# Four engine queues reordered around the attention add of a convolution-attention block with a quantised FFN, on one Trainium2 core

## The chip, the cores and the metric

One core of a Trainium2 chip runs the kernel. The time is device time in microseconds (us) of one execution, compared as a median over runs. In a profile, PE is TensorE, PEld its weight loads, DVE VectorE, ACT ScalarE, POOL GpSimd and SP the queue that issues the DMAs. Each engine works through its own list of instructions in order; semaphores join the lists.

## The reference

The input x is (16, 512, 24, 8): images, channels, rows, columns. Two blocks follow each other, each with a layer norm and a residual.

```python
def reference(x, fc1_w, fc2_w, sa_w, w1, w2):        # w1, w2: 2048 x 512 and 512 x 2048
    x = x + conv_attention(ln_over_channels(x))      # block 1
    t = tokens(x)                                    # (16, 192, 512)
    t = t + ffn(ln_over_last(t))                     # block 2
    return images(t)

def conv_attention(v):
    ca = sigmoid(mlp(mean_hw(v)) + mlp(max_hw(v)))   # mlp(a) = relu(a @ fc1.T) @ fc2.T
    v = v * ca                                       # gate of each channel
    s = conv7x7(concat(mean_c(v), max_c(v)), sa_w)
    return v * sigmoid(s)                            # gate of each token

def bitlinear(a, w):                                 # ternary weights, activations in 8 bits
    scale = 127 / max(max_abs_last(a), EPS)
    return (clip(round(a * scale)) / scale) @ ternary(w).T

def ffn(a):
    return bitlinear(gelu(bitlinear(a, w1)), w2)
```

## The kernel before

Two images make a pair: 384 tokens, three tiles of 128 tokens. There are eight pairs (NP = 8), and the loop's body c runs four stages of four pairs at once: FFN of `pair` = c (last tile) and of `nxt` = c + 1 (first two tiles), the normalisation of `nxt`, the channel and token gates of `att` = c + 2, and the turn into tokens and first statistics of `fresh` = c + 3. Bodies 0 to 4 have all of it; body 5 has no `fresh`, body 6 no `att` either, body 7 only the FFN of the last pair. A part before the loop prepares the weights and the first pairs.

The order of the work is written out by hand, once for each engine, in a `body` of each engine's block (POOL L513, ACT L695, DVE L1036, PE L1327). Nothing is reordered at run time. In one body the queues hold, in this case's names:

- DVE: `token_gate` and, for each tile of `nxt`, `add_attention` (L851: t = pv * gate + xt at L856, then statistics at L858 and L860) and `centre` (L862: cen = t - mean at L868, its largest magnitude at L869, then three tiny steps that need `rs2`, the reciprocal deviation that POOL makes, and give `q1`). For each tile `hidden_max` reads the Gelu's output twice, in halves (L883), `hidden_scale` makes `q2` (L891, L893), and `add_ffn` (L900) adds the FFN's product to t. For `att`: four `token_max` (L795), `hidden` (L802, L805) between the two small matrix products, `split_gate` (L815 to L818), three `scale_channels` (L824), `split_stats` (L837, L838) and, after the convolution on PE, `sum_conv` (L843). For `fresh`: `channel_stats` (L782) and `aggregate` (L788).
- POOL: `rstd2` (L452, L453) makes rs2; `round_x` (L477, L481) rounds cen once q1 is there; `round_g` (L488, two halves of 1024 columns, and L494) rounds the Gelu's output once q2 is there; `normalise1` (L458 to L466) makes v1 of `fresh` once DVE has aggregated its statistics.
- ACT: Gelu in four blocks of 512 columns, `pack_g` to f16 (two halves; after each SP issues a transposing DMA into hq), `token_mean` (after token_max), `copy_xq`, the two tanh gates, `sum_channels` (needed by split_stats) and copies out of PSUM. All its work is in the profile at L550.
- PE: `ffn_in` (L1190, four blocks of four 512-column matmuls), `ffn_out` (L1201, four quarters of four), the transposes `turn_x` (L1110), `turn_v1` (L1120), `turn_xq` (L1175, needs cen rounded) and `turn_res` (L1210), the small products `fc1` (L1130, needs all token_max and token_mean), `fc2` (L1136, needs `hidden`), `turn_ca` (L1143), `spread_ca` (L1152), and `conv` (L1166, 42 matmuls of 3 columns, needs split_stats).

In DVE's code a `link` issues an instruction and then waits for its end, a `chain.mark` only counts it, and `chain.wait()` waits for all counted ones:

```python
link(dve.scalar_tensor_tensor(t_tile, pv[par][:, s, :], sg[par][:, s:s + 1],   # L856
                              xt[par][:, s, :], ALU.mult, ALU.add))
link(dve.bn_stats(st2[:, :], t_tile))                                          # L858
wait(dve, rs2_ready, tile.at(1, -1))
dve.bn_aggr(mv2[tile.par][:, :], st2[:, :]).then_inc(stats2_ready, 1)          # L860
```

Of the kernel before, what the change touches and what calls it, by code (L numbers as in the profile page):

```python
# [5 lines left out]
def metaformer_kernel(nc, x, fc1_w, fc2_w, sa_w, w1, w2, out):  # L6
# [38 lines left out]
    with ctx:  # L45
# [340 lines left out]
        def _(pool):  # L386
# [126 lines left out]
            def body(pair, attend, normalise, turn, split):  # L513
# [6 lines left out]
                if normalise:  # L520
                    round_x(Tile(nxt, 0))
                round_g(Tile(pair, 2))
                if normalise:
                    rstd2(Tile(nxt, 1))
                    round_x(Tile(nxt, 1))
                    round_g(Tile(nxt, 0))
                    rstd2(Tile(nxt, 2))
                    round_x(Tile(nxt, 2))
# [12 lines left out]
        def _(act):  # L541
# [153 lines left out]
            def body(pair, attend, normalise, turn):  # L695
# [31 lines left out]
                if normalise:  # L727
                    gelu(Tile(nxt, 1), blocks=(0, 1))
                if attend:
                    copy_caT(att)  # L730
                if normalise:
                    gelu(Tile(nxt, 1), blocks=(2, 3))
# [5 lines left out]
                copy_out(Tile(pair, 1), OUT_BANK[2])  # L738
                if attend:
                    sum_channels(Tile(att, 2))  # L740
                if turn:
# [11 lines left out]
        def _(dve):  # L753
# [95 lines left out]
            def add_attention(tile):  # L849
# [6 lines left out]
                link(dve.scalar_tensor_tensor(t_tile, pv[par][:, s, :], sg[par][:, s:s + 1],  # L856
                                              xt[par][:, s, :], ALU.mult, ALU.add))
                link(dve.bn_stats(st2[:, :], t_tile))  # L858
# [141 lines left out]
            add_attention(Tile(pair0, 0))  # L1000
            centre(Tile(pair0, 0))
# [8 lines left out]
            add_attention(Tile(pair0, 1))  # L1010
            dve.wait_ge(w_turned, 8)
# [14 lines left out]
            add_attention(Tile(pair0, 2))  # L1026
            centre(Tile(pair0, 2))
# [8 lines left out]
            def body(pair, attend, normalise, turn):  # L1036
                nxt, att, fresh = pair.plus(1), pair.plus(2), pair.plus(3)

                if pair.c > 0:
                    add_ffn(Tile(pair.plus(-1), 2))  # L1040
                if normalise:
                    token_gate(nxt)
                    add_attention(Tile(nxt, 0))
                    centre(Tile(nxt, 0))
# [6 lines left out]
                hidden_scale(Tile(pair, 2))  # L1051
                if attend:
                    token_max(att, 2, V1_BANK[2])

                add_ffn(Tile(pair, 0))
                if normalise:
                    add_attention(Tile(nxt, 1))
# [3 lines left out]
                if normalise:  # L1061
                    hidden_max(Tile(nxt, 0), 0)
                    hidden_max(Tile(nxt, 0), 1)
                if attend:
                    hidden(att)
# [4 lines left out]
                if normalise:  # L1070
                    add_attention(Tile(nxt, 2))
                if attend:
                    split_gate(att)
                if normalise:
                    centre(Tile(nxt, 2))
                    hidden_max(Tile(nxt, 1), 0)
# [3 lines left out]
                if turn:  # L1080
                    channel_stats(fresh, 0, 1)
# [336 lines left out]
```

## Time and profile before

| | us |
|---|---|
| median of 3 runs (lowest, highest) | 311.19 (310.03, 312.21) |
| the profiled execution's own time | 311.29 |
| its span, first to last instruction | 309.3 |
| busy in the span: PE, DVE, ACT, POOL | 265.9, 249.7, 217.1, 165.6 |

The 2.0 us between the span and the execution's time lie outside the instructions. Rows of the trace are told in us from the span's start. A timeline row gives start, length, engine, line, operation, output and input, how many instructions it merges, and in brackets how long the engine had idled and who released it. An instruction's length on DVE or POOL contains any time in which it has begun and can't go on.

### The profile page before, as it was taken

The numbers are of one execution on the slowest core, as the hardware profiler recorded it, in microseconds if no ns is written. First come the engines' busy times: TensorE is split into PE (matmuls) and PEld (weight loads), VectorE is DVE, ScalarE is ACT, GpSimd is POOL, SyncE is SP. The second block draws the span as 40 slices with busy tenths as digits, with TensorE's granted clock in tenths as the row PEclk, the third lists the DMA queues.
The fourth block names the chain that finished last, engine by engine and source line by source line (L and its number), as shares of the span: only waits on it lengthen the run. The fifth ranks groups of instructions, "written<-read, shape, count | busy, mean of one in ns | idle before, by whom it ended". The sixth has DMA issues, their size and how long they took to land.

```text
span 309.3 us, 5830 instructions
## 1 busy us (share of the span) xinstructions
PE 265.9 (86%) x1826; PEld 153.4 (50%) x1834; DVE 249.7 (81%) x556; ACT 217.1 (70%) x442; POOL 165.6 (54%) x267
## 2 busy tenths in 40 slices
PE   2457659696699999999999999999999987999974
PEld 2345634564356465645565555555555544444431
DVE  0673889989699989998998999899989997788410
ACT  1863687579476978687778876787678846676831
POOL 9506655416855385648555765566656563346410
PEclk9999965969999999999999999999999999899998
DMA  7999100002253129412931393439223713073693
GB/s 202 389 392 401 45 1 0 2 2 57 42 141 70 24 46 246 96 34 54 252 72 35 69 237 70 37 69 256 53 50 72 151 39 68 17 174 72 74 209 102
DMA packets 71077, 34.19 MB, mean 111 GB/s; under 512 B 52040, under 2 KB 68424, under 8 KB 70536
## 3 DMA queue, kind: packets, MB, share of 16 engines
q1 hardware_dynamic: 69300, 32.78, 43.1%
q10 hardware_dynamic: 1748, 1.05, 1.2%
q8 instruction: 15, 0.25, 0.3%
q14 instruction: 14, 0.11, 0.1%
HBM read 14.94 MB, written 6.29 MB: 69 GB/s over the span
## 4 chain that ended last, share of the span: by engine, by line
DVE 40%; PE 36%; issue 10%; ACT 4%; POOL 4%; ACTq 2%; DMA 1%; another core or an unknown queue 1%; SPq 1%; DVEq 0%; POOLq 0%
PE ps_o L1201 12%; DVE amax L883 8%; PE ps_h L1190 6%; PE ps_t L1190 6%; DVE t L856 6%; PE front L1120 3%; DVE st L858 3%; DVE amax L869 3%; DVE pv L824 3%; PE small L1166 2%; DVE cen L868 2%; DVE junk_v L909 2%; DVE st L782 2%; PE front L1210 2%; DVE res L900 2%
## 5 line engine op out<-in xcount | busy, mean ns | idle before, releaser
L1201 PE MATMUL ps_o<-w2T,hq 128*128 128x512 f16 x384 | 92.7, 379 | 1.1 <-DMA hq<-w_raw 1.1
L488 POOL TENSOR_SCALAR w_room<-w_room,q 128x1024 f32<-128x1024 f32 x48 | 57.1, 1201 | 51.4 <-DVE q L893 50.9
L883 DVE TENSOR_REDUCE amax<-w_room 128x1 f32<-128x1024 f32 (+1 forms) x48 | 57.2, 1208 | 2.3 <-ACT w_room L550 2.2
L1190 PE MATMUL ps_h<-w1T,xq 128*128 128x512 f16 x208 | 54.0, 403 | 1.1 <-ACT xq L550 0.7
L1201 PEld LDWEIGHTS ps_o<-w2T,hq 128*128 128x128 f16 x384 | 36.3, 98 | 36.0 <-DMA hq<-w_raw 2.1
L550 ACT ACTIVATE w_raw<-w_room 128x1024 f16<-128x1024 f16 x48 | 50.4, 1052 | 0.6 <-POOL w_room L488 0.6
L550 ACT ACTIVATE w_room<-ps_h,s 128x512 f32<-128x512 f32 x52 | 35.0, 688 | 13.1 <-PE ps_h L1190 12.0
L1190 PE MATMUL ps_t<-w1T,xq 128*128 128x512 f16 x176 | 42.0, 382 | 0.0
L550 ACT ACTIVATE w_room<-ps_t,s 128x512 f32<-128x512 f32 x44 | 30.2, 687 | 8.0 <-PE ps_t L1190 5.6
L1190 PEld LDWEIGHTS ps_h<-w1T,xq 128*128 128x128 f16 x208 | 20.1, 103 | 23.9 <-issue 3.9
L550 ACT ACTIVATE junk_m<-front 128x192 bf16<-128x192 f32 x64 | 20.6, 332 | 14.7 <-DVE pooled L795 14.7
L900 DVE SCALAR_TENSOR_TENSOR res<-ps_o,s,t 128x512 f32<-128x512 f32 x24 | 18.0, 749 | 13.4 <-PE ps_o L1201 13.4
L477 POOL TENSOR_SCALAR cen<-cen,q 128x512 f32<-128x512 f32 x24 | 16.6, 692 | 20.4 <-DVE q L875 20.4
L1190 PEld LDWEIGHTS ps_t<-w1T,xq 128*128 128x128 f16 x176 | 17.1, 99 | 20.0 <-issue 1.1
L856 DVE SCALAR_TENSOR_TENSOR t<-pv,sg,xt 128x512 f32<-128x512 f32 x24 | 26.3, 1094 | 0.3
L1110 PE MATMUL front<-id,x_in 128*128 128x128 f32 x96 | 17.0, 314 | 7.7 <-DMA x_in<-in_x 5.8
L1120 PE MATMUL front<-id,v 128*128 128x128 f32 x96 | 18.2, 312 | 5.9 <-POOL v L465 3.8
L782 DVE BATCH_NORM_STATS2 st<-xt 128x6 f32<-128x512 f32 x24 | 15.5, 681 | 8.3 <-ACT xt L550 8.3
L550 ACT ACTIVATE w_room<-front 128x512 f32<-128x512 f32 x24 | 14.0, 585 | 8.8 <-PE front L1210 8.8
L795 DVE TENSOR_REDUCE pooled<-front 128x2 f32<-128x384 f32 x32 | 17.7, 552 | 2.5 <-PE front L1120 1.6
L465 POOL TENSOR_SCALAR v<-xt,minus_mean,rs 128x512 f32<-128x512 f32 x24 | 18.9, 788 | 1.4
L550 ACT ACTIVATE junk_p<-pv 128x512 bf16<-128x512 f32 x24 | 15.0, 626 | 6.0 <-DVE ch_stat L824 5.2
(125 smaller groups left out, 450.5 us busy)
## 6 DMA issues: line engine op xcount, KB each, us to landing
out<-w_room SPq DMA_DIRECT2D x16, 384.0 KB, 3.0
x_in<-in_x SPq DMA_DIRECT2D x14, 384.0 KB, 5.1
w_room<-in_L_ffn_w SPq DMA_DIRECT2D x4, 1024.0 KB, 8.8
w_raw<-in_L_ffn_w SPq DMA_DIRECT2D x4, 1024.0 KB, 12.0
x_in<-in_x ACTq DMA_DIRECT2D x2, 384.0 KB, 3.8
hq<-w_raw SPq DMA_TRANSPOSE x48, 3.1
fc_raw<-in_L_conv_fc_w ACTq DMA_DIRECT2D x2, 128.0 KB, 4.2
taps_rev<-in_L_conv_sa_w SPq DMA_DIRECT2D x1, 0.2 KB
```

What stands on the lines that cost most here:

```text
L465: pool.tensor_scalar(v1[:, s, :], xt[pair.par][:, s, :], minus_mean[:, s:s + 1], rs1[:, s:s + 1], ALU.add, ALU.mult).then_inc(normed, 1)
L488: pool.tensor_scalar(part, part, q2[tile.par][:, 0:1], MAGIC, ALU.mult, ALU.add).then_inc(g_rounded, 1)
L550: act.activation(out_ap, in_ap, func, **more).then_inc(signal, 1)
L782: chain.mark(dve.bn_stats(st1[:, s, :], xt[pair.par][:, s, :]))
L795: dve.tensor_reduce(pooled[:, k, 0:2], front[bank][:, 0:TOK].rearrange("p (i t) -> p i t", i=2), AX.X, ALU.max).then_inc(max_ready, 1)
L856: link(dve.scalar_tensor_tensor(t_tile, pv[par][:, s, :], sg[par][:, s:s + 1], xt[par][:, s, :], ALU.mult, ALU.add))
L883: chain.mark(dve.tensor_reduce(amax2[:, i:i + 1], w1_room[:, first + i * F // 2:first + (i + 1) * F // 2 + i], AX.X, ALU.max, apply_absolu ...
L900: dve.scalar_tensor_tensor(res[tile.par][:, :], ps_o[:, :], s2[tile.third][:, 0:1], t[tile.pair.par][:, tile.s, :], ALU.mult, ALU.add).the ...
L1110: last = pe.transpose(front[bank][:, tile_cols(k)], x_in[tile.pair.par][:, k, tile_cols(tile.s)], id32[:, :])
L1120: last = pe.transpose(front[bank][:, tile_cols(s)], v1[:, s, tile_cols(k)], id32[:, :])
L1190: last = pe.matmul(banks[b], xq[tile.pair.par][:, tile.s, k, :], w1T[:, k, b * 512:(b + 1) * 512], start=(k == 0), stop=(k == NC - 1))
L1201: last = pe.matmul(ps_o[:, :], hq[tile.par][:, k, :], w2T[:, k, :], start=(k == 0), stop=(k == NF - 1))
```

## The change

No instruction is added or taken away; their places in the four lists change, and DVE's attention add is split in two.

- `add_attention` only issues the add, counted and not waited for; its statistics become a step of their own, `row_stats`.
- DVE: the add of nxt's tile 1 goes from behind `hidden_scale(pair, 2)` and `add_ffn(pair, 0)` to ahead of both, with token_max 2 between it and its statistics; the add of tile 2 goes from behind `hidden_scale(nxt, 0)` to behind token_max 3, ahead of `hidden`, its statistics behind `hidden`, ahead of the second hidden_max of (nxt, 0). Of that tile's two hidden_max the first now goes ahead of `centre(nxt, 1)`. `split_gate` goes ahead of `hidden_scale(nxt, 0)`; scale_channels 0 and 1 go ahead of hidden_max(nxt, 1, 0), scale 2 ahead of channel_stats; `split_stats` goes ahead of hidden_max(nxt, 1, 1) and its scale; `add_ffn(pair, 2)` goes from the head of the next body to this body's end, ahead of aggregate(fresh, 2).
- POOL: rstd2 of tiles 1 and 2 go ahead of the round_g that stood before them.
- ACT and PE: two small steps trade places with a Gelu block, a copy, a block of ffn_in or a quarter of ffn_out. `turn_xq(nxt, 2)` on PE now stands behind the last quarter of ffn_out(pair, 2).

The diff, with some lines of context left out:

```diff
 # POOL, body
                     round_x(Tile(nxt, 0))
+                    rstd2(Tile(nxt, 1))
                 round_g(Tile(pair, 2))
                 if normalise:
-                    rstd2(Tile(nxt, 1))
                     round_x(Tile(nxt, 1))
+                    rstd2(Tile(nxt, 2))
                     round_g(Tile(nxt, 0))
-                    rstd2(Tile(nxt, 2))
                     round_x(Tile(nxt, 2))
 # ACT, body
-                    gelu(Tile(nxt, 1), blocks=(0, 1))
+                    gelu(Tile(nxt, 1), blocks=(0,))
                     copy_caT(att)
-                    gelu(Tile(nxt, 1), blocks=(2, 3))
+                    gelu(Tile(nxt, 1), blocks=(1, 2, 3))
                     sum_channels(Tile(att, 0))
                     sum_channels(Tile(att, 1))
                     pack_g(Tile(nxt, 0), 0)
+                    sum_channels(Tile(att, 2))
                 copy_out(Tile(pair, 1), OUT_BANK[2])
-                    sum_channels(Tile(att, 2))
 # DVE, add_attention
-                link(dve.scalar_tensor_tensor(t_tile, pv[par][:, s, :], sg[par][:, s:s + 1],
-                                              xt[par][:, s, :], ALU.mult, ALU.add))
-                link(dve.bn_stats(st2[:, :], t_tile))
+                chain.mark(dve.scalar_tensor_tensor(t_tile, pv[par][:, s, :], sg[par][:, s:s + 1],
+                                                    xt[par][:, s, :], ALU.mult, ALU.add))
+
+            def row_stats(tile):
+
+                chain.wait()
+                link(dve.bn_stats(st2[:, :], t[tile.pair.par][:, tile.s, :]))
                 wait(dve, rs2_ready, tile.at(1, -1))
                 dve.bn_aggr(mv2[tile.par][:, :], st2[:, :]).then_inc(stats2_ready, 1)
 # DVE, body
-                if pair.c > 0:
-                    add_ffn(Tile(pair.plus(-1), 2))
                     token_gate(nxt)
                     add_attention(Tile(nxt, 0))
+                    row_stats(Tile(nxt, 0))
                     centre(Tile(nxt, 0))
 ...
                 hidden_max(Tile(pair, 2), 1)
+                    add_attention(Tile(nxt, 1))
+                    token_max(att, 2, V1_BANK[2])
+                    row_stats(Tile(nxt, 1))
                 hidden_scale(Tile(pair, 2))
-                    token_max(att, 2, V1_BANK[2])
 
                 add_ffn(Tile(pair, 0))
-                    add_attention(Tile(nxt, 1))
+                    hidden_max(Tile(nxt, 0), 0)
                     centre(Tile(nxt, 1))
                     token_max(att, 3, V1_BANK[3])
-                    hidden_max(Tile(nxt, 0), 0)
+                    add_attention(Tile(nxt, 2))
+                    hidden(att)
+                    row_stats(Tile(nxt, 2))
                     hidden_max(Tile(nxt, 0), 1)
-                    hidden(att)
+                    split_gate(att)
                     hidden_scale(Tile(nxt, 0))
 
                 add_ffn(Tile(pair, 1))
-                    add_attention(Tile(nxt, 2))
-                    split_gate(att)
                     centre(Tile(nxt, 2))
-                    hidden_max(Tile(nxt, 1), 0)
                     scale_channels(Tile(att, 0), CA_BANK[0])
                     scale_channels(Tile(att, 1), CA_BANK[1])
+                    hidden_max(Tile(nxt, 1), 0)
+                    scale_channels(Tile(att, 2), CA_BANK[2])
                     channel_stats(fresh, 0, 1)
-                    scale_channels(Tile(att, 2), CA_BANK[2])
                     aggregate(fresh, 0, 1)
+                    split_stats(att)
                     hidden_max(Tile(nxt, 1), 1)
                     hidden_scale(Tile(nxt, 1))
-                    split_stats(att)
                     channel_stats(fresh, 2)
                     sum_conv(att)
+                add_ffn(Tile(pair, 2))
                     aggregate(fresh, 2)
 # PE, body
-                    ffn_in(Tile(nxt, 1), blocks=(0, 1))
+                    ffn_in(Tile(nxt, 1), blocks=(0,))
                     turn_ca(att)
-                    ffn_in(Tile(nxt, 1), blocks=(2, 3))
+                    ffn_in(Tile(nxt, 1), blocks=(1, 2))
                     a = spread_ca(Tile(att, 0), CA_BANK[0], a)
                     b = spread_ca(Tile(att, 1), CA_BANK[1], b)
+                    ffn_in(Tile(nxt, 1), blocks=(3,))
                 ffn_out(Tile(pair, 2), (0,))
 ...
                     b = turn_x(Tile(fresh, 2), X_BANK[2], b)
+                ffn_out(Tile(pair, 2), (3,))
                     a = turn_xq(Tile(nxt, 2), XQ_BANK[2], a)
-                ffn_out(Tile(pair, 2), (3,))
                     conv(att)
```

## Rows read from the trace of the kernel before

**Rows 1.** The page: busy time of the engines, and the chain that ended last

```profile
PE 265.9 (86%) x1826; PEld 153.4 (50%) x1834; DVE 249.7 (81%) x556; ACT 217.1 (70%) x442; POOL 165.6 (54%) x267
...
DVE 40%; PE 36%; issue 10%; ACT 4%; POOL 4%; ACTq 2%; DMA 1%; another core or an unknown queue 1%; SPq 1%; DVEq 0%; POOLq 0%
```

**Rows 2.** Stretches of bodies 1 to 5; busy us by engine, then granted clock

```profile
109.58:139.86 30.28, 29.44 (x210) 16.75 (x209) 28.34 (x64) 23.73 (x52) 18.21 (x31) 1.00 0.47 105
...
230.70:262.02 31.32, 28.48 (x198) 15.33 (x197) 28.00 (x59) 22.41 (x49) 17.50 (x28) 1.00 0.41 81
```

**Rows 3.** Timeline of VectorE, body 3

```profile
170.17 0.17 DVE L843 TENSOR_REDUCE conv_sum<-small 128x3 f32<-128x9 f32 x1 [0.72 <-PE small L1166]
...
172.95 0.52 DVE L868 TENSOR_SCALAR cen<-t,mv 128x512 f32<-128x512 f32 x1
...
174.80 0.55 DVE L795 TENSOR_REDUCE pooled<-front 128x2 f32<-128x384 f32 x1
...
179.22 0.74 DVE L900 SCALAR_TENSOR_TENSOR res<-ps_o,s,t 128x512 f32<-128x512 f32 x1
179.88 1.56 DVE L856 SCALAR_TENSOR_TENSOR t<-pv,sg,xt 128x512 f32<-128x512 f32 x1
...
184.28 0.55 DVE L795 TENSOR_REDUCE pooled<-front 128x2 f32<-128x384 f32 x1
...
188.25 1.17 DVE L856 SCALAR_TENSOR_TENSOR t<-pv,sg,xt 128x512 f32<-128x512 f32 x1
...
196.73 0.24 DVE L788 BATCH_NORM_AGGREGATE mv<-st 128x2 f32<-128x6 f32 x2
...
198.67 0.46 DVE L838 TENSOR_TENSOR ch_stat<-ch_stat 128x6 f32<-128x6 f32 x1
```

**Rows 4.** Timeline of GpSimd, body 3

```profile
170.77 0.19 POOL L458 TENSOR_SCALAR ve<-mv 128x1 f32<-128x1 f32 x1
...
173.27 0.59 POOL L453 TENSOR_TENSOR rs<-ve,half_pow 128x1 f32<-128x1 f32 x1
...
178.69 2.21 POOL L488 TENSOR_SCALAR w_room<-w_room,q 128x1024 f32<-128x1024 f32 x2 [2.46 <-DVE q L893]
...
187.76 2.64 POOL L488 TENSOR_SCALAR w_room<-w_room,q 128x1024 f32<-128x1024 f32 x2 [2.37 <-DVE q L893]
...
199.86 1.11 POOL L488 TENSOR_SCALAR w_room<-w_room,q 128x1024 f32<-128x1024 f32 x1
```

**Rows 5.** Timeline of VectorE, before the loop

```profile
40.33 0.70 DVE L868 TENSOR_SCALAR cen<-t,mv 128x512 f32<-128x512 f32 x1
```

**Rows 6.** Timeline of TensorE, body 3

```profile
185.69 0.61 PE L1130 MATMUL small<-pooled,fc1T 128*64 128x4 f32 x8
...
199.19 0.61 PE L1166 MATMUL small<-ch_stat,band 128*128 128x3 bf16 x18 [0.37 <-DVE ch_stat L838]
```

**Rows 7.** Timeline of VectorE, end of body 5

```profile
258.64 1.01 DVE L837 TENSOR_TENSOR ch_stat<-ch_stat 128x6 f32<-128x6 f32 x1 [0.22 <-ACT junk_p L550]
259.68 1.06 DVE L838 TENSOR_TENSOR ch_stat<-ch_stat 128x6 f32<-128x6 f32 x1
```

**Rows 8.** Timeline of GpSimd, end of body 5

```profile
258.51 2.21 POOL L488 TENSOR_SCALAR w_room<-w_room,q 128x1024 f32<-128x1024 f32 x2 [4.23 <-DVE q L893]
```

**Rows 9.** Timeline of TensorE, bodies 5 to 7

```profile
260.80 0.61 PE L1166 MATMUL small<-ch_stat,band 128*128 128x3 bf16 x18 [1.41 <-DVE ch_stat L838]
...
261.88 3.22 PE L1190 MATMUL ps_h<-w1T,xq 128*128 128x512 f16 x8
264.90 2.29 PE L1190 MATMUL ps_t<-w1T,xq 128*128 128x512 f16 x8
...
285.18 0.39 PE L1175 MATMUL front<-id,cen 128*128 128x128 f16 x4
...
286.27 1.89 PE L1190 MATMUL ps_h<-w1T,xq 128*128 128x512 f16 x8
```

**Rows 10.** A stretch of 1 us in body 6, columns as in rows 2

```profile
263.00:264.00 1.00, 1.00 (x3) 0.30 (x2) 0.96 (x2) 0.56 (x1) 0.00 (x0) 0.50 0.06 16
```

More of the change, by code:

```diff
@@ L737, in body @@
                     pack_g(Tile(nxt, 0), 0)
-                copy_out(Tile(pair, 1), OUT_BANK[2])
                 if attend:
                     sum_channels(Tile(att, 2))
+                copy_out(Tile(pair, 1), OUT_BANK[2])
                 if turn:
@@ L1000, in _ @@
             add_attention(Tile(pair0, 0))
+            row_stats(Tile(pair0, 0))
             centre(Tile(pair0, 0))
@@ L1010, in _ @@
             add_attention(Tile(pair0, 1))
+            row_stats(Tile(pair0, 1))
             dve.wait_ge(w_turned, 8)
@@ L1026, in _ @@
             add_attention(Tile(pair0, 2))
+            row_stats(Tile(pair0, 2))
             centre(Tile(pair0, 2))
@@ L1050, in body @@
                 hidden_max(Tile(pair, 2), 1)
-                hidden_scale(Tile(pair, 2))
+                if normalise:
+                    add_attention(Tile(nxt, 1))
                 if attend:
                     token_max(att, 2, V1_BANK[2])
+                if normalise:
+                    row_stats(Tile(nxt, 1))
+                hidden_scale(Tile(pair, 2))
                 add_ffn(Tile(pair, 0))
                 if normalise:
-                    add_attention(Tile(nxt, 1))
+                    hidden_max(Tile(nxt, 0), 0)
                     centre(Tile(nxt, 1))
@@ L1061, in body @@
                 if normalise:
-                    hidden_max(Tile(nxt, 0), 0)
+                    add_attention(Tile(nxt, 2))
+                if attend:
+                    hidden(att)
+                if normalise:
+                    row_stats(Tile(nxt, 2))
                     hidden_max(Tile(nxt, 0), 1)
                 if attend:
-                    hidden(att)
+                    split_gate(att)
                 if normalise:
@@ L1070, in body @@
                 if normalise:
-                    add_attention(Tile(nxt, 2))
-                if attend:
-                    split_gate(att)
-                if normalise:
                     centre(Tile(nxt, 2))
-                    hidden_max(Tile(nxt, 1), 0)
                 if attend:
@@ L1079, in body @@
                     scale_channels(Tile(att, 1), CA_BANK[1])
-                if turn:
-                    channel_stats(fresh, 0, 1)
+                if normalise:
+                    hidden_max(Tile(nxt, 1), 0)
                 if attend:
@@ L1084, in body @@
                 if turn:
+                    channel_stats(fresh, 0, 1)
                     aggregate(fresh, 0, 1)
+                if attend:
+                    split_stats(att)
                 if normalise:
@@ L1088, in body @@
                     hidden_scale(Tile(nxt, 1))
-                if attend:
-                    split_stats(att)
                 if turn:
@@ L1099, in _ @@
                 body(Pair(c), c < NP - 2, c < NP - 1, c < NP - 3)
-            add_ffn(Tile(Pair(NP - 1), 2))
         @block.tensor
@@ L1379, in body @@
                     b = spread_ca(Tile(att, 1), CA_BANK[1], b)
+                if normalise:
+                    ffn_in(Tile(nxt, 1), blocks=(3,))
                 ffn_out(Tile(pair, 2), (0,))
```

## The prediction

> **What bounds the kernel now.** I began with the page's chain of work that ended last: DVE has 40% of it and PE 36% [rows 1], so no single engine sets the time. The stretches by body say why. A full body takes 30.28 us, with DVE busy 28.34 and PE 29.44 in it; bodies 1 to 4 are alike within 0.02, so the loop is steady, and only body 5 is longer, 31.32 [rows 2]. PE's busy time covers waits between pipelined matmuls, so I read the timelines next, of body 3, and looked for lengths that the work doesn't explain. The reader should see three things there. DVE's only marked idle time is 0.72 before sum_conv, where it waits for the convolution, whose own start waited 0.37 for DVE's split_stats [rows 3, 6]. The add of attention takes 1.56 for tile 1 and 1.17 for tile 2, though add_ffn, as many elements with one operand in PSUM, takes 0.74 [rows 3]. Both lie beside a round_g of GpSimd (178.69 to 180.90, 187.76 to 190.40), and the second add stretches that round_g from 2.21 to 2.64 in return [rows 4]. So the add and a GpSimd instruction over SBUF exclude each other: the later one waits for the other's end. The add's 1.56 ends 0.54 behind round_g's end, so 0.54 is what it needs once let in.
>
> **What one full body saves.** The add of tile 1 moves ahead of hidden_scale(pair, 2), which releases the first round_g: 1.56 - 0.74 = 0.82. That of tile 2 moves ahead of hidden_scale(nxt, 0): 1.17 - 0.74 = 0.43. split_stats moves ahead of a hidden_max, so the POOL work that stretched L838 to 0.46 [rows 3] comes later; a tiny step such as sum_conv takes 0.17: 0.29. The wait before sum_conv, 0.72, goes, since hidden_max, hidden_scale and channel_stats now stand between split_stats and it. In four places the queue no longer waits for its last instruction to end (two adds, the hidden_max ahead of the first of them, statistics of tile 1). Unlinked, add_ffn lets its successor start 0.66 behind its own start, 0.08 before it ends [rows 3]; with the restart I take 0.11 each, 0.45. Sum: 2.71.
>
> **What the same body pays.** Five new waits, in the order of DVE's queue.
>
> First, centre of nxt's tile 0 needs rs2. GpSimd works from the statistics of fresh's first tiles (196.73 + 0.24 [rows 3]) to the end of round_g(nxt, 1) at 200.97, 4.0; then from 170.77 to 173.86, 3.1, through fresh's third tile to rs2 [rows 4]. DVE takes 200.45 - 196.73 = 3.7 from those statistics to sum_conv, which is 170.17 a body later, and 174.80 - 170.17 - 0.58 (three tiny steps) = 4.05 more until it wants rs2 [rows 3]: 7.8 against POOL's 7.4, so it is hidden now. With 0.72 and 0.29 gone DVE is there after 6.7. POOL is not sooner, and the add of tile 0 now runs into the end of round_g(nxt, 1) and then blocks POOL for its 0.54. Late by 0.7 to 1.2: I take 0.9.
>
> Second, centre of tile 1. Counted from the start of token_max 2, its row statistics end after 1.4, rstd2 after 2.3, and round_g(pair, 2), now behind both, covers 2.4 to 3.5 and 3.5 to 4.6. DVE has hidden_max(nxt, 0, 0) ahead of centre; that waits for two Gelu blocks behind a token_mean, 2.55, some 0.15 of which is a wait, and takes 1.13: cen starts at 3.7, just inside the second half. Is cen (one operand, 0.52 alone in the loop [rows 3]) shut out like the add? Before the loop one cen beside normalise1 took 0.70 [rows 5]. That bounds the wait by 0.2 below and by the add's 0.82 above; I take 0.68, cen's end at 4.6 + 0.27 against 3.7 + 0.49, since 0.70 shows a real wait. The Trainium skill ("SBUF — State Buffer", "SBUF: two separate sides") says that a VectorE instruction in a two-port mode, not only one with two SBUF inputs, shares a port pair with GpSimd under a lock held for a whole instruction. By that rule the wait is the rest of the POOL instruction, as taken; by the smallest row alone it would be 0.2. The trace agrees in kind, with that 0.70; that a cen waits out a whole round_g half no row of before shows.
>
> Third, token_max 3 to hidden. fc1 started 185.69 - 184.28 = 1.41 behind the start of token_max 3 and took 0.61 [rows 3, 6]; hidden can't start sooner than 2.0 behind it. Two hidden_max lay between; now one add does, with token_max 0.46 + 0.66 + 0.15 for running into round_x. DVE waits 0.65 to 0.75: 0.7. The add's 0.15 is the fourth. Fifth, centre of tile 2 starts 0.7 behind the release of round_g(nxt, 0), first half 1.1: 0.25 (0 to 0.8). With the 0.15 for Gelu the sum is 0.9 + 0.15 + 0.68 + 0.7 + 0.15 + 0.25 = 2.83.
>
> So 2.71 goes and 2.83 comes: bodies 0 to 4 keep their length, within 0.5 either way. PE and ACT have no say: PE's work, about 28.6 without waits, hides behind DVE's queue; if it doesn't, turn_xq(nxt, 0), which needs cen rounded some 1.3 later than now, costs up to 0.6. The transposing DMAs of (pair, 2) start 2 us later but are used some 10 us later.
>
> **What the end saves.** In body 5 split_stats took 1.01 and 1.06 beside the round_g at 258.51, not 0.17 twice [rows 7, 8], and PE sat idle 1.41 until conv [rows 9]. Now split_stats goes ahead of the hidden_scale that releases this round_g, and of a hidden_max. PE's wait goes, 1.41, and split_gate, ahead of hidden_scale, gives PE some 0.3 more: 1.7 (1.0 to 2.2). Behind that idle time the granted clock read 0.50, the lower level of 1.2 GHz [rows 10]: sixteen matmuls in body 6 took 3.22 + 2.29, while eight at 2.4 GHz take 1.89 [rows 9], that is 1.7 too long. Without the idle time, 1.65 back. Against this stands one place in body 6: turn_xq came 1.09 before the ffn_in that needs its copy, with a quarter of ffn_out (0.87) between [rows 9]. That quarter now comes first and no conv follows: PE waits 0.87 (0 to 0.9).
>
> **Sum.** 311.29 - 1.7 - 1.65 + 0.87 = 308.8 against the profiled execution's own time, 311.29 (span 309.3 and 2.0 around it), which stands 0.1 above the median of the runs, 311.19. A measurement of this kernel can tell about 1%, 3.1 us.
>
> **The rivals.** (1) The savings stay: cen of tile 1 slips in between the halves of round_g (it misses by 0.2), and the convolution keeps DVE waiting enough to hide rs2. Then a body gains 0.7 + 0.2 or so, five of them 4.5: 304.3. For it: the margin is small and the lengths repeat to 0.02, so it holds in every body or in none. Against it: all three spans hang on the same token_max. (2) Nothing comes at the end: body 5 becomes bound by something else (the gate's path through fc2, the sum over channels on ACT behind a pack_g now ahead of it) and PE idles long enough for the low clock all the same. Then 311.3 to 312.2. The change does then not do what it can. (3) Slower: the low clock in every full body. PE will wait about 0.45 for turn_xq(nxt, 1) and as long for token_mean 3, with four short transposes between and fc1's 0.61 behind. Row 260.80 shows 1.41 idle ahead of the narrow conv followed by the low level; 0.37 ahead of the same conv was not [rows 6, 9]. If the new gap is enough, five bodies lose 1.65 each, 8.2: 317. [...]
>
> **How the numbers follow.** Forecast, no more than 1% gained: 0.45, 308.8 with a range of its own of 306.8 to 310.8. Rival 1: 0.2. Rival 2: 0.2. Rival 3: 0.1. A smaller loss, by 0.4 a body: 0.05. The range of 8 in 10 cuts off half of rival 1 and all of rival 3: 304.4 to 312.6. Faster by over 1% (under 308.1): rival 1 and a third of the forecast, 0.36. Slower by over 1% (over 314.3): rival 3 and a little, 0.11. Within 1%: 0.53.
>
> **What would show it.** In the profile after: L856 at 0.74 to 0.95 throughout; cen of tile 1 at over 1.0; the wait of L872 for rs2 at some 0.9 and that of L802 for fc1 at 0.7 in every full body; no idle time before sum_conv; bodies still 30.3. In body 5 L837 and L838 short, conv released by PE's own order, 16 matmuls of body 6 in 3.5 and a wait of 0.9 for ACT's xq ahead of body 7. Wrong, if bodies are under 29.8 or over 30.8, or if the clock falls elsewhere.

## The result and the profile after

The changed kernel takes 312.19 us (median of 15 runs) against 311.38 for the kernel before (15 runs on the same chip): a ratio of 1.0045, 95% interval 1.0027 to 1.0063. That is slower by 0.45%, and 3.4 us above the forecast of 308.8. The profiled execution took 312.81, its span 310.8.

From the page of the kernel after, busy time by engine and the chain that ended last, as in [rows 1]:

```profile
PE 266.3 (86%) x1834; PEld 154.6 (50%) x1834; DVE 251.8 (81%) x556; ACT 217.3 (70%) x442; POOL 163.4 (53%) x267
...
DVE 49%; PE 20%; issue 13%; ACT 8%; POOL 4%; ACTq 2%; DMA 1%; SPq 1%; DVEq 0%; POOLq 0%
```

The page shows next to nothing: the same busy time, with a chain that runs more through DVE and less through PE. The stretches between two starts of sum_conv, which is where I divide the bodies, show where the time went. Bodies 0, 3 and 5 after, columns as in [rows 2]:

```profile
78.23:111.17 32.94, 30.14 (x205) 17.08 (x204) 27.57 (x66) 23.24 (x51) 17.48 (x31) 0.95 0.30 65
...
172.46:203.10 30.64, 29.45 (x211) 16.94 (x209) 28.73 (x65) 23.75 (x53) 17.77 (x31) 1.00 0.46 104
...
233.78:263.50 29.72, 28.07 (x197) 15.25 (x195) 26.81 (x61) 21.99 (x50) 15.74 (x27) 1.00 0.37 81
```

Cut in the same way, body 0 before takes 31.35 and bodies 1 to 5 are those of [rows 2]. Against before, body 0 is 1.59 longer, bodies 1 to 4 are 0.37 longer each (1.49 together), body 5 is 1.60 shorter, and all behind it is 0.06 longer: 1.5 in all, the difference of the spans. Three of these were forecast at other values: body 0 and bodies 1 to 4 at no change, what lies behind body 5 at 0.78 shorter.

The timeline of VectorE in body 3 after, to be read against [rows 3]:

```profile
173.27 0.88 DVE L847 TENSOR_SCALAR sg<-sg_tanh 128x3 f32<-128x3 f32 x1
...
175.92 0.74 DVE L872 TENSOR_SCALAR cen<-t,mv 128x512 f32<-128x512 f32 x1
...
181.20 0.74 DVE L856 SCALAR_TENSOR_TENSOR t<-pv,sg,xt 128x512 f32<-128x512 f32 x1
...
184.36 1.22 DVE L887 TENSOR_REDUCE amax<-w_room 128x1 f32<-128x1024 f32 x1 [0.16 <-ACT w_room L550]
185.50 1.23 DVE L872 TENSOR_SCALAR cen<-t,mv 128x512 f32<-128x512 f32 x1
...
188.53 0.94 DVE L856 SCALAR_TENSOR_TENSOR t<-pv,sg,xt 128x512 f32<-128x512 f32 x1
190.11 0.15 DVE L802 TENSOR_SCALAR hid_r<-small 64x4 f32<-64x4 f32 x1 [0.65 <-PE small L1140]
...
192.51 0.17 DVE L815 TENSOR_SCALAR ca_row<-ca_tanh 128x8 f32<-128x8 f32 x1
...
194.01 0.92 DVE L872 TENSOR_SCALAR cen<-t,mv 128x512 f32<-128x512 f32 x1
...
200.85 0.17 DVE L838 TENSOR_TENSOR ch_stat<-ch_stat 128x6 f32<-128x6 f32 x1
...
203.10 0.15 DVE L843 TENSOR_REDUCE conv_sum<-small 128x3 f32<-128x9 f32 x1
```

Beside it GpSimd, as in [rows 4]:

```profile
173.02 1.11 POOL L488 TENSOR_SCALAR w_room<-w_room,q 128x1024 f32<-128x1024 f32 x1
...
184.23 2.22 POOL L488 TENSOR_SCALAR w_room<-w_room,q 128x1024 f32<-128x1024 f32 x2
...
193.53 2.38 POOL L488 TENSOR_SCALAR w_room<-w_room,q 128x1024 f32<-128x1024 f32 x2 [1.34 <-DVE q L897]
```

The reader is to see that the savings are there: the adds of tiles 1 and 2 take 0.74 and 0.94 (0.20 of the second is the new wait that the forecast has as its fourth), L838 takes 0.17, sum_conv waits for nothing. In their place the cen of the three tiles takes 0.74, 1.23 and 0.92, hidden waits 0.65, and token_gate, three elements a partition, takes 0.88 where it took 0.16 in the kernel before: it starts 0.25 into the half round_g at 173.02 and ends with it, 174.15 against 174.13. By the Trainium skill ("SBUF — State Buffer", "SBUF: two separate sides") a VectorE instruction in a two-port mode waits out a GpSimd instruction whole. The rows agree for the step of three elements, and for the cen of tile 1, which ends at 186.73, 0.28 behind round_g's end at 186.45; that these instructions run in such a mode no row shows.

TensorE in body 3 after, as in [rows 6], and then from the end of body 5 on, as in [rows 9]:

```profile
176.44 0.55 PE L1130 MATMUL front<-id,v 128*128 128x128 f32 x3 [0.48 <-POOL v L465]
...
188.99 0.40 PE L1185 MATMUL front<-id,cen 128*128 128x128 f16 x4 [0.54 <-POOL cen L477]
189.48 0.60 PE L1140 MATMUL small<-pooled,fc1T 128*64 128x4 f32 x8
...
262.03 0.38 PE L1185 MATMUL front<-id,cen 128*128 128x128 f16 x4 [0.25 <-ACT w_room L550]
262.25 0.60 PE L1176 MATMUL small<-ch_stat,band 128*128 128x3 bf16 x18
...
263.32 1.89 PE L1200 MATMUL ps_h<-w1T,xq 128*128 128x512 f16 x8
265.05 1.89 PE L1200 MATMUL ps_t<-w1T,xq 128*128 128x512 f16 x8
...
278.19 0.40 PE L1185 MATMUL front<-id,cen 128*128 128x128 f16 x4 [0.46 <-POOL cen L477]
...
287.71 1.90 PE L1200 MATMUL ps_h<-w1T,xq 128*128 128x512 f16 x8 [0.69 <-ACT xq L550]
```

Here are two waits that the kernel before did not have: 0.48 for v and 0.54 for the cen of tile 1, ahead of fc1. Those of before, 0.37 for split_stats [rows 6] and 0.21 each for ca_row and for ch_stat, are gone. The latter two, from body 3 of the kernel before:

```profile
190.92 0.40 PE L1143 MATMUL small<-idb,ca_row 128*128 128x128 bf16 x4 [0.21 <-DVE ca_row L818]
...
194.55 0.63 PE L1210 MATMUL front<-id,res 128*128 128x128 f32 x4 [0.21 <-DVE ch_stat L824]
```

Per body 0.79 goes and 1.02 comes.

The mean granted clock of the 15 runs of the changed kernel goes from 0.949 to 0.970, so executions of one and the same kernel differ in how long they run at the lower level, and part of the difference between two profiles is chance. In the profile after the clock fell in body 0, on the matmuls behind this wait:

```profile
83.33 0.55 PE L1130 MATMUL front<-id,v 128*128 128x128 f32 x3 [2.35 <-POOL v L465]
83.71 2.68 PE L1211 MATMUL ps_o<-w2T,hq 128*128 128x512 f16 x8
```

The granted clock from 85 to 88 us was 0.50, and VectorE waited 0.55 and 0.51 for TensorE's transpositions there. In the profile before the same wait lasted 2.36 and the clock stayed at 1.00. Of the profiles of e1 to e12 below, only that of e8 has the lower level at this place; in the others it lies in the first 5 us of body 0. So I put 1.06 of body 0's 1.59 down to that execution, which is argued and not shown; the 0.53 left is near the 0.37 of the other bodies.

### The profile page after: what moved, and what is told of

It is laid out like the page before. It is cut to its first block, busy times and chain, and to the rows that moved or that the text cites. A ratio compares the mean times of both kernels' runs of the same rounds, so it can differ in the third digit from the quotient of the medians.

```text
span 310.8 us, 5852 instructions
## 1 busy us (share of the span) xinstructions
PE 266.3 (86%) x1834; PEld 154.6 (50%) x1834; DVE 251.8 (81%) x556; ACT 217.3 (70%) x442; POOL 163.4 (53%) x267
## 4 chain that ended last, share of the span: by engine, by line
DVE 49%; PE 20%; issue 13%; ACT 8%; POOL 4%; ACTq 2%; DMA 1%; SPq 1%; DVEq 0%; POOLq 0%
DVE amax L887 9%; DVE cen L872 6%; PE ps_o L1211 6%; DVE amax L873 4%; DVE t L856 4%; DVE pooled L795 3%; DVE st L782 3%; ACT w_room L550 3%; DVE pv L824 2%; DVE st L862 2%; POOL cen L477 2%; PE small L1146 2%; DVE junk_v L913 2%; PE ps_t L1200 2%; PE ps_t L1247 2%
## 5 line engine op out<-in xcount | busy, mean ns | idle before, releaser
L1211 PE MATMUL ps_o<-w2T,hq 128*128 128x512 f16 x384 | 93.7, 383 | 1.3 <-DMA hq<-w_raw 1.3
L488 POOL TENSOR_SCALAR w_room<-w_room,q 128x1024 f32<-128x1024 f32 x48 | 55.0, 1157 | 29.9 <-DVE q L897 28.7
L1211 PEld LDWEIGHTS ps_o<-w2T,hq 128*128 128x128 f16 x384 | 37.0, 99 | 37.2 <-DMA hq<-w_raw 1.8
L1200 PEld LDWEIGHTS ps_h<-w1T,xq 128*128 128x128 f16 x208 | 19.4, 102 | 22.7 <-issue 2.7
L452 POOL TENSOR_SCALAR ve<-mv 128x1 f32<-128x1 f32 x24 | 5.2, 216 | 40.4 <-DVE mv L864 39.7
L1130 PE MATMUL front<-id,v 128*128 128x128 f32 x96 | 18.9, 321 | 8.7 <-POOL v L465 6.1
L856 DVE SCALAR_TENSOR_TENSOR t<-pv,sg,xt 128x512 f32<-128x512 f32 x24 | 22.0, 916 | 0.3
L1130 PEld LDWEIGHTS front<-id,v 128*128 128x128 f32 x96 | 13.1, 163 | 16.4 <-POOL v L465 7.9
L872 DVE TENSOR_SCALAR cen<-t,mv 128x512 f32<-128x512 f32 x24 | 20.6, 858 | 0.3
```

The costliest lines, as they stand in the source:

```text
L488: pool.tensor_scalar(part, part, q2[tile.par][:, 0:1], MAGIC, ALU.mult, ALU.add).then_inc(g_rounded, 1)
L856: chain.mark(dve.scalar_tensor_tensor(t_tile, pv[par][:, s, :], sg[par][:, s:s + 1], xt[par][:, s, :], ALU.mult, ALU.add))
L872: link(dve.tensor_scalar(c[:, :], t_tile, mv2[tile.par][:, 0:1], None, ALU.subtract))
L1130: last = pe.transpose(front[bank][:, tile_cols(s)], v1[:, s, tile_cols(k)], id32[:, :])
L1200: last = pe.matmul(banks[b], xq[tile.pair.par][:, tile.s, k, :], w1T[:, k, b * 512:(b + 1) * 512], start=(k == 0), stop=(k == NC - 1))
L1211: last = pe.matmul(ps_o[:, :], hq[tile.par][:, k, :], w2T[:, k, :], start=(k == 0), stop=(k == NF - 1))
```

## The experiments

**Theory A**: VectorE's queue bounds a body. The adds no longer run into GpSimd's round_g, but token_gate and the cen of tiles 1 and 2 now do, the add of tile 2 runs into round_x (188.24 to 188.93), and hidden waits for fc1; each of these waits counts in full. **Theory B**: TensorE's changed order (turn_xq behind the last quarter of ffn_out) sets the lengths. The kernel before, run beside the first four, had a median of 311.58.

**e1.** TensorE's order alone undone.

```diff
-                ffn_out(Tile(pair, 2), (3,))
                 if normalise:
                     a = turn_xq(Tile(nxt, 2), XQ_BANK[2], a)
+                ffn_out(Tile(pair, 2), (3,))
```

> The changed kernel with turn_xq(nxt, 2) put back ahead of the last quarter of ffn_out(pair, 2) on TensorE, all else as changed. Theory A (the loss lies in VectorE's queue: token_gate and the centring steps shut out by GpSimd's instructions, and hidden waiting for fc1): a full body stays at 30.65 us, only TensorE's wait of 0.7 to 0.85 ahead of body 7 goes, so about 0.8 us less in all, 311.3. Theory B (TensorE's new order bounds the bodies: its waits for v1, for cen rounded and for fc1): every body shortens, 30.3 or less, 310 or less in all.

Measured: 312.62, ratio 1.0044 (1.0021 to 1.0068). Bodies 1 to 4 stay at 30.64 to 30.68, so theory B falls for the loop as it was stated. The order is not without effect, though: TensorE's 0.48 for v goes, and 0.67 for ScalarE comes ahead of its turn_xq of tile 2. The wait ahead of body 7 goes, but the gain is given back: two waits of TensorE grow, at the end of body 5 and in body 6.

```profile
261.07 0.38 PE L1185 MATMUL front<-id,cen 128*128 128x128 f16 x4 [1.11 <-ACT w_room L550]
278.51 0.40 PE L1185 MATMUL front<-id,cen 128*128 128x128 f16 x4 [1.07 <-POOL cen L477]
```

**e2.** centre of tile 1 back ahead of the first hidden_max.

```diff
                 if normalise:
+                    centre(Tile(nxt, 1))
                     hidden_max(Tile(nxt, 0), 0)
-                    centre(Tile(nxt, 1))
```

> The changed kernel with centre(nxt, 1) back ahead of the first hidden_max of (nxt, 0), so that cen is made before round_g(pair, 2) starts. Theory A: cen of tile 1 falls from 1.23 to 0.5 us, the 0.16 wait for Gelu goes too, a body shortens by 0.7 to 0.9 to about 29.8, 308 in all; hidden's wait of 0.65 stays. If cen and round_g start within 0.1 us of each other and round_g wins, cen is 1.2 or longer and nothing is gained. Theory B (VectorE's stalls are slack that TensorE covers): body within 0.1 of 30.65.

Measured: 306.58, ratio 0.9856 (0.9826 to 0.9885), faster than both kernels. Bodies of 29.80 to 29.84, 0.84 shorter. VectorE and TensorE in body 3:

```profile
181.05 0.48 DVE L872 TENSOR_SCALAR cen<-t,mv 128x512 f32<-128x512 f32 x1
...
186.20 0.15 DVE L802 TENSOR_SCALAR hid_r<-small 64x4 f32<-64x4 f32 x1 [1.00 <-PE small L1140]
```

```profile
173.37 0.55 PE L1130 MATMUL front<-id,v 128*128 128x128 f32 x3 [0.48 <-POOL v L465]
...
185.21 0.39 PE L1185 MATMUL front<-id,cen 128*128 128x128 f16 x4
185.53 0.63 PE L1140 MATMUL small<-pooled,fc1T 128*64 128x4 f32 x8
```

The cen gets in before round_g, and TensorE's wait of 0.54 for it is gone. The number is theory A's, but VectorE now waits 1.00 for fc1, which does not look like a queue that bounds.

**e3.** centre of tile 2 ahead of hidden_scale(nxt, 0) and add_ffn(pair, 1).

```diff
                 if normalise:
+                    centre(Tile(nxt, 2))
                     hidden_scale(Tile(nxt, 0))
                 add_ffn(Tile(pair, 1))
-                if normalise:
-                    centre(Tile(nxt, 2))
```

> The changed kernel with centre(nxt, 2) ahead of hidden_scale(nxt, 0) and add_ffn(pair, 1), so that cen is made before round_g(nxt, 0) is released. Theory A: cen of tile 2 falls from 0.92 to 0.5 us, a body shortens by 0.4 to about 30.2, 310.2 in all. Theory B: no change, 312.2.

Measured: 311.23, ratio 1.0006 (0.9983 to 1.0028); bodies of 30.45, shorter by 0.2. Half of what VectorE saves in cen (0.92 to 0.48) reaches the body. A new wait for TensorE's spread stands behind it, 0.16:

```profile
191.48 0.48 DVE L872 TENSOR_SCALAR cen<-t,mv 128x512 f32<-128x512 f32 x1
...
196.89 0.69 DVE L824 CUSTOM_DVE_ANT_0 pv<-v,front 128x512 f32<-128x512 f32 x1 [0.16 <-PE front L1161]
```

**e4.** round_g of tile 1 not halved: whole, behind the next body's rstd2, out of token_gate's way.

```diff
-                    round_g(Tile(pair, 1), (1,))
+                    round_g(Tile(pair, 1))
...
-                    round_g(Tile(nxt, 1), (0,))
```

> The changed kernel with GpSimd's first half of round_g(nxt, 1) taken from between the two normalise1 of a body and put with the other half, behind rstd2 of the next body's first tile. Theory A: token_gate falls from 0.88 to 0.17 us and cen of tile 0 from 0.74 to about 0.5, a body shortens by 0.9 to about 29.7, 308 in all; price: ACT packs that half about 1 us later, which its idle time before token_mean 0 (0.9) covers. Theory B: no change or slower, since the packing comes later, 312.2 to 314.

Measured: 314.51, ratio 1.0113 (1.0076 to 1.015). token_gate fell to 0.14 as expected, the cen of tile 0 stayed at 0.74, and the body grew to 31.16. ScalarE packs what round_g makes, and its next copy, which frees a bank of TensorE's, comes later with it. ScalarE and TensorE:

```profile
178.07 1.06 ACT L549 ACTIVATE w_raw<-w_room 128x1024 f16<-128x1024 f16 x1 [1.60 <-POOL w_room L488]
```

```profile
179.76 0.52 PE L1129 MATMUL front<-id,v 128*128 128x128 f32 x3 [1.53 <-ACT w_room L549]
```

After these four came **theory D**: the body is TensorE's work, 29.2 to 29.5, and what TensorE itself waits for. Its waits depend on the other engines in a ring: v from GpSimd, which follows VectorE's channel_stats; the rounded cen of tile 1, which follows VectorE's centre; then fc1, on which VectorE's hidden and so its later channel_stats wait. A VectorE step counts if it lies on that ring, not otherwise. **Rival C**: the new tail of VectorE's queue is what costs, not the adds.

**e5.** The early adds undone, with them the new places of the Gelu's first hidden_max and of GpSimd's rstd2; the tail, split_gate's new place, ScalarE's and TensorE's orders kept. The edit, with parts left out:

```diff
-                    add_attention(Tile(nxt, 1))
...
                 add_ffn(Tile(pair, 0))
                 if normalise:
-                    hidden_max(Tile(nxt, 0), 0)
+                    add_attention(Tile(nxt, 1))
+                    row_stats(Tile(nxt, 1))
                     centre(Tile(nxt, 1))
...
                 add_ffn(Tile(pair, 1))
                 if normalise:
+                    add_attention(Tile(nxt, 2))
+                    row_stats(Tile(nxt, 2))
                     centre(Tile(nxt, 2))
```

> The early adds undone (adds of tiles 1 and 2, their statistics, the Gelu parts and GpSimd's rstd2 stand as in the kernel before); the new tail of VectorE's queue, ScalarE's and TensorE's orders stay as in the changed kernel. Theory A (the early adds cost because they push token_gate's followers, cen of tiles 1 and 2, add 2 and hidden into GpSimd's or fc1's way; the tail saves 0.72 + 0.29 + 0.22 a body and pays 0.93 for token_gate and cen of tile 0): bodies 30.0, L856 back to 1.56 and 1.17, cen of tiles 1 and 2 at 0.5, hidden without a wait, body 5 some 1.3 shorter than before; 308.3 us. Rival C (the tail is what costs, by token_gate's 0.71 and a late split_gate): bodies 30.6 or more, time 312 or more.

Measured: 317.14, ratio 1.0193 (1.0153 to 1.0232), bodies of 31.59: missed by far, by a flaw of the experiment. Without the add of tile 2 ahead of it, split_gate comes too early for ScalarE's ca_tanh:

```profile
193.69 0.17 DVE L815 TENSOR_SCALAR ca_row<-ca_tanh 128x8 f32<-128x8 f32 x1 [2.06 <-ACT ca_tanh L550]
```

**e6.** The tail undone, the early adds kept.

```diff
+                if pair.c > 0:
+                    add_ffn(Tile(pair.plus(-1), 2))
...
+                    hidden_max(Tile(nxt, 1), 0)
                 if attend:
                     scale_channels(Tile(att, 0), CA_BANK[0])
...
-                if attend:
-                    split_stats(att)
                 if normalise:
                     hidden_max(Tile(nxt, 1), 1)
                     hidden_scale(Tile(nxt, 1))
+                if attend:
+                    split_stats(att)
...
-                add_ffn(Tile(pair, 2))
```

> The new tail undone (hidden_max of tile 1's first half, split_stats and the add_ffn of tile 2 stand as in the kernel before); the early adds, ScalarE's and TensorE's orders stay as in the changed kernel. Theory A: the adds save 0.82 + 0.43 + 0.2 a body and pay 0.74 (cen 1), 0.65 (hidden), 0.15 (Gelu), 0.2 (add 2), 0.43 (cen 2), so bodies are 30.28 + 0.5 to 0.7 = 30.8 to 31.0, token_gate 0.17 again, cen of tile 0 0.5; body 5 saves nothing: 314 us. Rival C (the tail costs): bodies under 30.3, 310 to 311 us with the end as before.

Measured: 314.0, ratio 1.0086 (1.0057 to 1.0115), bodies of 30.85: 0.56 above the kernel before, 0.2 above the changed one. The adds cost, the tail saves a little; rival C falls. A miss: body 5 stays short, 29.83.

**e7.** hidden_max behind token_max 3, so that fc1 is released sooner.

```diff
                 if normalise:
-                    hidden_max(Tile(nxt, 0), 0)
                     centre(Tile(nxt, 1))
                 if attend:
                     token_max(att, 3, V1_BANK[3])
                 if normalise:
+                    hidden_max(Tile(nxt, 0), 0)
                     add_attention(Tile(nxt, 2))
```

> On the changed kernel the first hidden_max of (nxt, 0) goes behind token_max 3, so centre of tile 1 stands two steps sooner and token_max 3 releases fc1 1.1 us sooner for hidden. Theory A (each wait is worth its length as long as VectorE's queue bounds a body): cen of tile 1 at 0.5 as in the run with centre alone moved, and hidden's wait, 1.00 there, goes to 0.1 or less: bodies 29.80 - 0.9 = 28.9, or 29.1 if TensorE's own work, some 28.6 with 0.48 for turn_v1, sets the length; 302.5 us. Rival D (what is left is bound by something else, GpSimd's chain through round_g or TensorE): bodies stay 29.7 to 29.8, and a wait of 0.9 turns up elsewhere in VectorE's queue; 306.5 us.

Measured: 306.52, ratio 0.9844 (0.9811 to 0.9878), bodies of 29.83: no shorter than e2. token_max 3 came 1.12 sooner (182.87 against 183.99 in e2) and hidden's wait is unchanged, because fc1 stands in TensorE's queue behind matmuls that start at 182.63 and leave no gap. First VectorE, then TensorE:

```profile
186.20 0.15 DVE L802 TENSOR_SCALAR hid_r<-small 64x4 f32<-64x4 f32 x1 [1.00 <-PE small L1140]
```

```profile
182.63 2.75 PE L1211 MATMUL ps_o<-w2T,hq 128*128 128x512 f16 x12
185.22 0.39 PE L1185 MATMUL front<-id,cen 128*128 128x128 f16 x4
185.53 0.63 PE L1140 MATMUL small<-pooled,fc1T 128*64 128x4 f32 x8
```

**e8.** e7 with centre of tile 2 moved as in e3.

> As the run before it, and centre of (nxt, 2) ahead of hidden_scale of (nxt, 0), so that its cen lies ahead of the round_g that hidden_scale releases. Theory A: cen of tile 2 at 0.5 in place of 0.92, another 0.2 to 0.4 a body: bodies 28.5 to 28.9, 301 us. Rival D: as the run before it within 0.3 us, since VectorE no longer bounds the body or waits elsewhere.

Measured: 307.3, ratio 0.9871 (0.9827 to 0.9916), bodies of 29.63. In this stretch, behind hidden, 0.2 reaches the body as in e3, while TensorE's wait for v falls from 0.51 to 0.30. The whole time is no shorter than e7's.

**e9.** e5 with split_gate also where it was: of VectorE's order only the tail is left.

> As the run with the early adds undone, and split_gate behind the add of tile 2 as in the kernel before; of VectorE's order only the new tail is left. In that run split_gate waited 2.06 for ScalarE's ca_tanh in a body of 31.59. Theory A (each of VectorE's waits counts in full): 31.59 - 2.06 = 29.5 a body, 305.5 us or less. Theory D (a body is TensorE's work, 29.2 to 29.45, and what TensorE itself waits for): before, its waits were 0.21 for ca_row, 0.21 for the res of the spread and 0.37 for the convolution; without the last and with 0.2 to 0.5 for v the body is 29.9 to 30.3 and the time 309 to 311 us. Rival C (the tail costs): bodies over 30.4.

Measured: 309.98, ratio 0.9966 (0.9936 to 0.9996), bodies of 30.20. Theory A's 29.5 is refuted, D's range holds it. TensorE's waits in body 3:

```profile
174.21 0.55 PE L1128 MATMUL front<-id,v 128*128 128x128 f32 x3 [0.29 <-POOL v L465]
...
190.98 0.40 PE L1151 MATMUL small<-idb,ca_row 128*128 128x128 bf16 x4 [0.42 <-DVE ca_row L818]
```

**e10.** e2 with work added for VectorE ahead of hidden.

```diff
                     add_attention(Tile(nxt, 2))
+                    link(dve.tensor_reduce(amax1[:, :], t[nxt.par][:, 1, :], AX.X, ALU.max,
+                                           apply_absolute_value=True))
```

> The run with centre of tile 1 moved back (306.58 us, bodies of 29.80, VectorE waiting 1.00 for fc1 ahead of hidden), with one reduction over 128x512 more ahead of hidden, which is work added that changes no output: 0.69 and 0.08 for its link. Theory A (VectorE's queue bounds the body): 29.80 + 0.77 = 30.57 a body, 310.5 us. Theory D (TensorE's order sets the moment of fc1): hidden's wait falls to 0.25, bodies stay 29.8, 306.6 to 307.4 us.

Measured: 306.89, ratio 0.9865 (0.9822 to 0.9908); bodies of 29.81 where e2 has 29.80. The added reduction lies whole in the wait:

```profile
185.17 0.68 DVE L1073 TENSOR_REDUCE amax<-t 128x1 f32<-128x512 f32 x1
186.31 0.15 DVE L802 TENSOR_SCALAR hid_r<-small 64x4 f32<-64x4 f32 x1 [0.46 <-DVE amax L1073]
```

hidden starts 16.87 behind sum_conv (169.44), in e2 16.81 (169.39). The row names the added reduction as releaser, but that ends at 185.85; fc1 ends at 186.21, 0.10 ahead of hidden:

```profile
185.58 0.63 PE L1142 MATMUL small<-pooled,fc1T 128*64 128x4 f32 x8
```

This is the clearest of the runs: with centre back, VectorE's queue does not bound the stretch ahead of hidden.

**e11.** e2 with v sooner: the third tile's statistics ahead of hidden_scale(nxt, 1), its normalise1 ahead of the half round_g.

```diff
                     normalise1(fresh, 0, 1)
-                    round_g(Tile(nxt, 1), (0,))
                     normalise1(fresh, 2)
+                    round_g(Tile(nxt, 1), (0,))
...
+                if turn:
+                    channel_stats(fresh, 2)
+                if normalise:
                     hidden_scale(Tile(nxt, 1))
                 if turn:
-                    channel_stats(fresh, 2)
+                    aggregate(fresh, 2)
```

> The same run with the third tile's channel statistics ahead of hidden_scale(nxt, 1) on VectorE and its normalise1 ahead of the half round_g on GpSimd, so that TensorE gets v some 1.2 us sooner. Theory D: TensorE's only wait in a body, 0.51 for v, goes: 29.80 - 0.51 = 29.3 a body, 304 us. Theory A: VectorE gets nothing from it (sum_conv 0.2 later): bodies 29.8 to 30.0, 306.6 to 307.6 us. A third way: the half round_g comes 1.2 us later and the packing behind it, and TensorE waits at its second transposition of v as it did when round_g was moved whole: bodies over 30.

Measured: 306.08, ratio 0.9838 (0.9789 to 0.9886), bodies of 29.74. Theory D's 29.3 was not reached. The wait for v went, and a wait of the kind that the expectation names as its third way took most of its place, without the body going over 30: TensorE's third transposition of v waits for ScalarE, and cen of tile 0 runs into the round_g that now comes later. TensorE, then VectorE:

```profile
177.81 0.52 PE L1131 MATMUL front<-id,v 128*128 128x128 f32 x3 [0.29 <-ACT junk_m L550]
```

```profile
172.08 1.32 DVE L872 TENSOR_SCALAR cen<-t,mv 128x512 f32<-128x512 f32 x1
```

**e12.** e11 with centre of tile 2 moved as in e3.

> The same with centre of tile 2 moved as well (bodies of 29.63 with a wait of 0.30 for v in TensorE). Theory D: 29.63 - 0.30 = 29.3 a body, no shorter than the run beside it, 304 to 305 us. Theory A: VectorE saves 0.2 to 0.4 more than the run beside it.

Measured: 306.72, ratio 0.9863 (0.9821 to 0.9905), bodies of 29.73: as e11, which is D's side, though its 29.3 was not reached here either. e2, e7, e8, e10, e11 and e12 all beat both kernels; their intervals overlap, so they are not ranked.

TensorE's account of one full body, from the stretches and timelines (marked waits are those in brackets; what is left, 0.06 to 0.17, are gaps too short to be marked):

| kernel | PE busy | its marked waits | sum | body |
|---|---|---|---|---|
| before | 29.44 | 0.21 ca_row, 0.21 ch_stat, 0.37 split_stats | 30.23 | 30.29 |
| after | 29.45 | 0.48 v, 0.54 cen 1 | 30.47 | 30.64 |
| e1 | 29.34 | 0.54 cen 1, 0.67 ACT | 30.55 | 30.64 |
| e2 | 29.25 | 0.48 v | 29.73 | 29.81 |
| e3 | 29.46 | 0.29 v, 0.54 cen 1 | 30.29 | 30.46 |
| e4 | 29.18 | 1.53 ACT, 0.38 cen 1 | 31.09 | 31.16 |
| e6 | 29.45 | 0.38 cen 1, 0.48 ch_stat, 0.41 split_stats | 30.72 | 30.85 |
| e9 | 29.35 | 0.29 v, 0.42 ca_row | 30.06 | 30.20 |
| e11 | 29.33 | 0.29 ACT | 29.62 | 29.74 |

That busy and idle time add up is no proof. What the table shows is that the work stays within 0.3 while the named waits make the differences (e5, e7, e8, e10 and e12, read in the same way, leave 0.11 to 0.14). That the cen of tile 1 costs is shown by e2, and that VectorE has slack ahead of hidden once it is back, by e7 and e10. That the changed kernel itself is bound in the same way is read from its waits.

## Why the prediction was wrong

**The step that failed** is "PE and ACT have no say: PE's work, about 28.6 without waits, hides behind DVE's queue", and with it "So 2.71 goes and 2.83 comes: bodies 0 to 4 keep their length". No row gives the 28.6: PE was busy 29.44 in a body of 30.28 [rows 2], and with the 0.79 of waits that the timeline marks 0.05 was left over. I took some of that busy time for hidden waits; the best versions found here still have 29.2 to 29.3 of it. So at most about 1 us of a body was to be had, whatever VectorE saved, and the right question for each new wait was whether TensorE feels it. The cen of tile 1 it feels, 0.54 ahead of fc1: moving that one step back is worth 0.84 a body (e2). The prediction priced this cen, but set the price against savings on VectorE that TensorE could not use. Of the 4.0 between the forecast and the profiled execution (312.81), 1.59 lie in body 0, 1.49 in bodies 1 to 4, 0.10 in body 5 and 0.84 behind it.

**The sizes of the new waits were close.** Forecast against measured: 0.9 and 0.93 from sum_conv to the first token_max (5.56 after, 4.63 before); Gelu 0.15 and 0.16; cen of tile 1 0.68 and 0.74 (1.23 less 0.49); hidden 0.7 and 0.65; add of tile 2 0.15 and 0.20; cen of tile 2 0.25 and 0.43. The 0.13 by which split_gate comes late was not foreseen: the hidden_max ahead of it ends at 192.38, ScalarE's ca_tanh at 192.49, and L815 starts at 192.51. The sum paid is 3.24 instead of 2.83, so VectorE's own account, too, comes out longer: 0.12 was forecast, 0.37 measured. The mis-sized term there is the fifth, cen of tile 2. It waits out what is left of the first half of round_g, as forecast, but it starts 0.48 into that half, which ends at 194.64, so that 0.63 is left where the forecast had 0.4; cen ends 0.29 behind it, at 194.93.

**The first wait had another cause.** I foresaw centre of tile 0 late by 0.9 for rs2. It is not late for it: rs2 is there at 177.34 and wanted at 177.44. Instead token_gate is shut out by the half round_g for 0.71 and cen of tile 0 for 0.22 by GpSimd's v. That the total agrees is chance. The forecast's own sum does not come out either: GpSimd's two stretches, 4.0 and 3.1, make 7.1 and not 7.4. Nor was the wait worth its length: VectorE still comes 0.16 too early for the Gelu behind it (184.36).

**Body 5** came as forecast: 1.60 shorter, 1.7 said. TensorE's marked waits there fell from 2.67 (0.74, 0.21, 0.31, 1.41) to 1.48 (0.48, 0.54, 0.21, 0.25), by 1.19. Most of the other 0.41 is in where the body is cut: sum_conv starts 0.55 behind TensorE's next ffn_in at the head of body 5 (233.78 and 233.23) and 0.18 behind it at the end (263.50 and 263.32). So the number came out with another make-up: 1.41, 0.53 for ca_row and 0.27 of smaller waits went, and 1.02 came, for v and for the cen of tile 1, that was not counted. Nor does the gain hang on split_stats alone: with the tail undone body 5 is short as well (e6), since there split_stats takes 0.17 at 263.91 all the same. With the tail and without the early split_gate (e9) body 5 takes 31.49. There TensorE waits 1.34 for ca_row, and the granted clock reads 0.50 from 252 to 254 us behind it:

```profile
251.44 0.42 PE L1151 MATMUL small<-idb,ca_row 128*128 128x128 bf16 x4 [1.34 <-DVE ca_row L818]
```

Some 1.9 of that length is the clock: eight matmuls of ffn_in take 3.63 there (251.67 to 255.30), and 1.72 in the kernel after (254.49 to 256.21). Apart from the clock, then, body 5 is short with either early place alone, and ScalarE's and TensorE's orders, which e6 and e9 both keep, are not ruled out as the reason.

**Behind body 5** the 1.65 came back as forecast: 16 matmuls took 3.45 in place of 5.14. It may be a gain only against executions in which the lower clock falls there: the runs of before lie at 310.0 to 310.3 (6 of 15) or at 311.2 and more, but only one, at 311.29, was profiled, so that the quicker ones lack it is not shown. The 0.87 ahead of body 7 was right, 0.85: turn_xq starts 1.08 ahead of that ffn_in, 0.23 being its own (0.69 is marked as idle). Missed was TensorE's wait of 0.46 for the cen of tile 1 in body 6, whose rounding on GpSimd (277.01) took 1.12 in place of 0.69 beside an add (276.83). From the end of the 16 matmuls to the ffn_in of body 7 TensorE takes 20.94 (266.77 to 287.71) where it took 19.25 (267.02 to 286.27): 0.85, 0.46 and 0.38 of smaller gaps, so all of the 1.69 is given back.

**The rivals.** Rival 1 fell at its own condition, the cen that slips in ahead of round_g; where an edit made it do so (e2), a body gained 0.47 on the kernel before, not 0.9. Rival 2 is not what happened, for the end did gain. Rival 3 fell: the clock stays at 1.00 in bodies 1 to 5, with TensorE's wait of 0.54 in each. The smaller loss of 0.4 a body is what the loop does; it had a chance of 0.05, since I let two equal sums cancel.

**Left open:** which executions get the lower clock, and where, and which part of the change shortens body 5. Neither was tried.

## What to carry to other kernels

When two engines are both busy for over 90% of a loop's body, write the account of each (busy, plus its marked waits, against the length) before pricing an edit on one of them. Here the smaller remainder, TensorE's 0.84, came near what the best versions gained on the kernel before, 0.47 to 0.65 a body. A step moved out of one lock's way puts its neighbours into it, so look at which instruction stands beside the long GpSimd one afterwards, and above all whether the result that another engine waits for is among them. Test for slack directly: add work to the engine that you believe bounds, and see whether the loop notices.

## What the hardware showed that was not expected

A step of three elements a partition (token_gate, 0.16 in the kernel before) took 0.88 beside a round_g half, while a reduction over 1024 elements ran its usual 1.22 beside another round_g (184.36, with GpSimd's 184.23 to 186.45): here it was the short step that was shut out. And equal idle time is not followed by an equal clock: after 2.36 of waiting the granted clock read 1.00 in the profile before, after 2.35 it read 0.50 in the profile after.
